# Graph attention in a decoder kernel: value weighting and normalisation moved between VectorE, ScalarE and GpSimd

## The reference, cut to what matters

```python
def _L2_attn_ref(h, Wl, Wr, att_l, att_r, Wf, ln_gamma, ln_beta):
    fl = (h @ Wl.T).reshape(b, n, H, HD).transpose(0, 2, 1, 3)      # H = 8, HD = 32
    fr = (h @ Wr.T).reshape(b, n, H, HD).transpose(0, 2, 1, 3)
    sl = einsum('bhnd,d->bhn', leaky(fl), att_l[0])
    sr = einsum('bhnd,d->bhn', leaky(fr), att_r[0])
    p = softmax(sl[:, :, :, None] + sr[:, :, None, :], axis=-1)
    ctx = einsum('bhnm,bhmd->bhnd', p, fr)
    y = h + ctx.transpose(0, 2, 1, 3).reshape(b, n, d) @ Wf.T
    mu, var = mean(y, -1), mean(square(y - mu), -1)
    return (y - mu) * rsqrt(var + 1e-05) * ln_gamma + ln_beta
x = x + _L2_attn_ref(layernorm(x), ...)
```

## Time and profile before

| what | value |
|---|---|
| median of 3 runs | 3631.68 us (3626.03 to 3635.91) |
| the profiled execution's own time | 3622.71 us |
| its span | 3620.9 us |
| TensorE busy in the whole span | 3182.0 us, 88% |
| VectorE | 1830.8 us, 51% |
| ScalarE | 1200.6 us, 33% |
| GpSimd | 917.2 us, 25% |
| mean granted TensorE clock | 0.939 |

### The profile page before, as it was taken

The page is one execution under the profiler, slowest core; times in us unless marked ns, Lnnn a source line. Parts: engine busy times, 40 slices in busy tenths (PEclk is TensorE's granted clock), DMA queues, the critical chain, the costliest instruction groups (busy, mean ns, idle before and its releaser), DMA issues. The chain is left out here.

```text
span 3620.9 us, 75209 instructions
## 1 busy us (share of the span) xinstructions
PE 3182.0 (88%) x30384; PEld 2203.4 (61%) x30384; DVE 1830.8 (51%) x4577; ACT 1200.6 (33%) x2371; POOL 917.2 (25%) x754
## 2 busy tenths in 40 slices
PE   8886999999977868878778999789996999899978
PEld 3334555555666854746545555489996886566655
DVE  7886544543233554332586666543334662455543
ACT  1222333333223432311225655322221652244332
POOL 1001533432000000423427878412111110104000
PEclk9998999999989989978889999889998999999989
DMA  4223000001042020634601110278886100111100
GB/s 150 58 67 97 9 9 17 8 8 32 18 55 24 4 52 4 182 99 125 180 18 33 34 30 21 76 269 333 332 323 222 38 8 6 61 49 53 42 9 15
DMA packets 173918, 287.21 MB, mean 79 GB/s; under 512 B 79120, under 2 KB 144197, under 8 KB 164274
## 3 DMA queue, kind: packets, MB, share of 16 engines
q1 hardware_dynamic: 166130, 262.48, 23.5%
q0 software_dynamic: 7488, 20.46, 1.7%
HBM read 244.49 MB, written 28.48 MB: 75 GB/s over the span
## 5 line engine op out<-in xcount | busy, mean ns | idle before, releaser
L2646 PE MATMUL ps<-L_ffn_xsT,arena 128*128 128x128 f32 x2584 | 309.9, 279 | 20.1 <-DVE L_ffn_xsT L2445 14.1
L2646 PEld LDWEIGHTS ps<-L_ffn_xsT,arena 128*128 128x128 f32 x2584 | 301.8, 196 | 23.8 <-DVE L_ffn_xsT L2445 16.8
L161 POOL TENSOR_TENSOR rstd<-nsc,mhalf 112x4 f32<-112x4 f32 (+1 forms) x24 | 40.1, 1669 | 919.6 <-DVE nsc L154 918.7
L820 POOL TENSOR_TENSOR L_xattn_rn<-L_xattn_ss,mhalf 125x16 f32<-125x16 f32 (+1 forms) x64 | 185.8, 2903 | 257.2 <-DVE L_xattn_ss L883 257.2
L3329 POOL TENSOR_TENSOR L_xattn_pT<-L_xattn_pT,L_xattn_keep 125x678 int32<-125x678 int32 x128 | 190.4, 1510 | 71.6 <-ACT L_xattn_pT L3584 71.6
L2544 ACT ACTIVATE L_ffn_silu<-ps,arena 128x128 f32<-128x128 f32 x280 | 102.9, 368 | 268.9 <-PE ps L2646 253.6
L701 PE MATMUL ps<-L_attn_prod,arena 128*32 128x448 f32 (+29 forms) x672 | 157.8, 507 | 27.3 <-DVE L_attn_prod L510 27.0
L2454 DVE SCALAR_TENSOR_TENSOR L_ffn_hT<-ps,arena,L_ffn_silu 128x128 f32<-128x128 f32 x280 | 97.9, 350 | 155.6 <-ACT L_ffn_silu L2544 155.4
L997 PE MATMUL ps<-arena,L_xattn_cT 128*125 128x512 f32 x384 | 166.1, 592 | 0.0
L2323 POOL DMA_INDIRECT L_ffn_rows_out<-L_ffn_ys,L_ffn_dest x78 | 79.7, 1022 | 335.5 <-DVE L_ffn_ys L2463 303.7
L2659 PE MATMUL ps<-arena,L_ffn_hT 128*128 128x256 f32 x646 | 154.1, 383 | 0.1
(11 more groups left out here) (585 smaller groups left out, 6873.1 us busy)
## 6 DMA issues: line engine op xcount, KB each, us to landing
arena<-in_L_ffn_up SPq DMA_DIRECT2D x35, 2056.0 KB
arena<-in_L_ffn_down SPq DMA_DIRECT2D x35, 1152.0 KB
L_xattn_ctxT<-in_ctxT SPq DMA_DIRECT2D x48, 375.0 KB, 3.7
arena<-in_L_ffn_up SPq DMA_DIRECT2D x43, 384.0 KB
L_attn_a<-L_attn_skew SPq DMA_DIRECT2D x16, 784.0 KB, 5.1
L_xattn_ctx<-in_ctx SPq DMA_DIRECT2D x30, 375.0 KB
arena<-L_xattn_kp SPq DMA_DIRECT2D x64, 93.8 KB, 3.3
L_xattn_mask<-in_mask SPq DMA_DIRECT2D x32, 164.1 KB, 8.4
```

Source lines behind the costliest of these rows:

```text
L820: nc.gpsimd.tensor_tensor(rn[0:r, i], ss[0:r, i], core.mhalf[0:r, 0:H], ALU.pow).then_inc(po_r.step("root", i), 1)
L2646: ins = nc.tensor.matmul(ps[:, 2 + b % 4, half * TS:(half + 1) * TS], self.up(i % WU, k, half * HM + m), xsT[:, i % 2, k], start=(k == 0), ...
```

## The change

Three things are moved in the second part of `L2Graph`, the rest of the program is as it was.

- `weighed(c)` goes from VectorE to GpSimd.
- The normalisation is split in three. ScalarE reads y from PSUM and computes `y * root - mean * root` into `yn` (L3136 in the changed kernel, one instruction for each batch, with two operands of one number per token). GpSimd multiplies `yn` by gamma (L2976). VectorE adds `yn` to `x` (L3055).
- For ScalarE's offset VectorE writes `minus`, the mean times -1 (L3048), behind the epsilon, and GpSimd multiplies it by the root into `less` (L2971).

TensorE's list keeps its order. Its waits now name other engines: `numerators(c)` waits for GpSimd's `weighed(c)`, and `result(c)` waits for ScalarE's read of the bank, `yn(c-3)`.

```diff
+            def weighed(c):
+                f = 2 * c // NH
+                pool.wait_ge(ac_w.sem, ac_w.at(f, "exp"))
+                pool.wait_ge(ac_r.sem, ac_r.at(2 * c + 1, "fr"))
+                if c >= 2:
+                    pool.wait_ge(pe_n.sem, pe_n.at(c - 2, "num"))
+                nc.gpsimd.tensor_tensor(by_head(wf[:, c % 2]), fr[:, 2 * c:2 * c + 2, :].rearrange("p n (h d) -> p (n h) d", d=HD),
+                                        pair_of(wa[:, :, 0], c), ALU.mult).then_inc(po_w.step("weighed"), 1)
+
+            def roots(c):
                 ln.pool(pool, ve_y, po, c)
+                if c >= 2:
+                    pool.wait_ge(ac_y.sem, ac_y.at(c - 2, "yn", 1))
+                pool.wait_ge(ve_y.sem, ve_y.at(c, "minus"))
+                pool.wait_ge(po.sem, po.at(c, "lnrs"))
+                nc.gpsimd.tensor_tensor(less[:, c % 2], minus[:, c % 2], ln.rs[:, :], ALU.mult).then_inc(po.step("lnmr"), 1)
+
+            def gains(c):
+                for u in range(2):
+                    pool.wait_ge(ac_y.sem, ac_y.at(c, "yn", u))
+                    nc.gpsimd.tensor_tensor(yn[:, c % 2, u * D:(u + 1) * D], yn[:, c % 2, u * D:(u + 1) * D], self.gam, ALU.mult).then_inc(po_g.step("gain", u), 1)
+            weighed(0)
+            weighed(1)
+            for c in range(PAIRS + 2):
+                if 2 <= c + 1 < PAIRS:
+                    weighed(c + 1)
+                if 0 <= c - 2:
+                    gains(c - 2)
+                if 0 <= c - 1 < PAIRS:
+                    roots(c - 1)
...
             def statistics(c):
                 bank = OUT[c % 3]
                 ln.vector(dve, ve_y, c, lambda u, q: ps[0:T, bank, u * D:(u + 1) * D], lambda u: dve.wait_ge(pe_o.sem, pe_o.at(c, "out")))
+                if c >= 2:
+                    dve.wait_ge(po.sem, po.at(c - 2, "lnmr"))
+                nc.vector.tensor_scalar(minus[:, c % 2], ln.mv[:, :, 0], -1.0, None, ALU.mult).then_inc(ve_y.step("minus"), 1)
 
             def result(c):
-                bank = OUT[c % 3]
-                dve.wait_ge(po.sem, po.at(c, "lnrs"))
-                for u in range(2):
-                    nc.vector.scalar_tensor_tensor(out=yn[:, c % 2, u * D:(u + 1) * D], in0=ps[0:T, bank, u * D:(u + 1) * D], scalar=ln.mv[:, u, 0:1], in1=self.gam,
-                                                   op0=ALU.subtract, op1=ALU.mult).then_inc(ve_a.step("gain", u), 1)
                 for u in range(2):
                     x = core.x[0:T, 2 * c + u, :]
-                    dve.wait_ge(ve_a.sem, ve_a.at(c, "gain", u))
+                    dve.wait_ge(po_g.sem, po_g.at(c, "gain", u))
                     dve.wait_ge(po_b.sem, po_b.at(2 * c + u, "shift"))
-                    nc.vector.scalar_tensor_tensor(out=x, in0=yn[:, c % 2, u * D:(u + 1) * D], scalar=ln.rs[:, u:u + 1], in1=x,
-                                                   op0=ALU.mult, op1=ALU.add).then_inc(ve_a.step("out", u), 1)
+                    nc.vector.tensor_tensor(x, x, yn[:, c % 2, u * D:(u + 1) * D], ALU.add).then_inc(ve_a.step("out", u), 1)
...
-            weighed(0)
             for c in range(PAIRS + 2):
                 if c < PAIRS:
                     contexts(c)
-                if c + 1 < PAIRS:
-                    weighed(c + 1)
...
+            def results(c):
+                bank = OUT[c % 3]
+                act.wait_ge(po.sem, po.at(c, "lnmr"))
+                if c >= 2:
+                    act.wait_ge(ve_a.sem, ve_a.at(c - 2, "out", 1))
+                for u in range(2):
+                    nc.scalar.activation(yn[:, c % 2, u * D:(u + 1) * D], ps[0:T, bank, u * D:(u + 1) * D], ACT.Identity,
+                                         bias=less[:, c % 2, u:u + 1], scale=ln.rs[:, u:u + 1]).then_inc(ac_y.step("yn", u), 1)
+            for c in range(PAIRS + 1):
+                if c < PAIRS:
+                    contexts(c)
                 if c == 1:
                     exps(1)
+                if c >= 1:
+                    results(c - 1)
```

## The result

| | before | after |
|---|---|---|
| median of 20 runs each | 3631.42 us (3626.03 to 3638.37) | 3638.98 us (3625.59 to 3654.31) |
| ratio after to before | | 1.0023 (95%: 1.0013 to 1.0032) |
| profiled execution, own time | 3622.71 | 3641.36 |
| its span, granted clock | 3620.9, 0.939 | 3639.3, 0.941 |

The kernel became 7.6 us slower (0.23%, just inside the 0.3% told of above; by the interval of the ratio it is 4.7 to 11.6 us); 3639.7 had been forecast. The profiled spans differ by more, 18.4 us: 7.4 of it is there before `L2Graph` begins (1795.85 before, 1803.21 after, in unchanged code), and some 4 us come after it. So the stage is compared by itself, from TensorE's first transposes of it to the first L197 of the next stage on VectorE, in three pieces.

A forecast was written before the change was run, and what follows sets the result against it. VectorE was taken to bound the loop's middle at 4.66 us a round; a dependent chain would replace it. Loop 11.7 us more, beginning 3.8 less: 8 slower, 3631.7 + 8 = 3639.7 us, range 3630 to 3648.

The forecast's parts named there:

- the loop: First statistics of y to the stage's end: eight chains plus 0.8 us, 50.7 for 39.0, 11.7 us more.
- the beginning: Up to the first statistics of y: 2.8 us from the unwaited first context, 1.5 from TensorE's clock.
- the first part: Up to the last sum by head: two early weightings over products L2967 lose about 0.5 us.
- the signs named: VectorE idle 2 to 3 us, L3041 6 to 6.5 apart, L2962 1.27, first context unwaited, TensorE idle about 2.
- The round: Pair loop: one chain from statistics to statistics, 6.5 us with a weighting and 5.8 without, against 4.66 before.
- What the weighting costs: GpSimd between root and gamma, pairs 0 to 4: 1.27 us, covering ScalarE's reads; without it one read, 0.55.
- Contention: VectorE's first addition to x beside GpSimd's second gamma product: 0.27 us per pair, bounds nothing and 0.39.
- Rival A: GpSimd's weighting is dear, its repeated operand costing as much again: 14 us slower, 3646; chance 0.17.
- Rival B: TensorE's clock falls inside the loop; half the pairs hit makes it 16 us slower, 3648; chance 0.06.
- Rival D: GpSimd's weighting isn't really ahead; TensorE waits under 1 us a round, inside slack, 3640 still; chance 0.04.
- Rival C: Pair loop: chain is covered, TensorE's 4.31 us round becomes the bound, 5 us faster, 3626; chance 0.11.
- The 0.36 in brackets: TensorE's wait for VectorE's context in its 4.67 us round before the change, leaving its own round 4.31.

The follow-up runs named there:

- norm late: Statistics first, with the seven small next-stage-mean instructions moved behind pair 6's addition: 3624.53 us against 3631.98 before, ratio 0.9983; repeated, 0.9979.
- statistics first: Changed kernel, with VectorE taking pair c-1's statistics ahead of pair c-2's addition to x: 3631.33 us against 3634.68 before, ratio 0.9992.

## Why the prediction was right

The forecast of 3639.7 us was 0.7 us from the median, and the mechanism is the one that it named: rounds one after another, each a closed chain. The terms were off in ways that partly cancel: the loop was forecast 2.8 us too long, the beginning gave 0.8 less than forecast, and the first part lost 1.1 more, which is not shown to come from the change. So the mechanism and the direction were earned, but a miss of 0.7 us is closer than the terms were, and closer than an interval of 4.7 to 11.6 us can tell: that much of it is luck. Of the signs named, VectorE's idle time (2.19) and the first context without a wait came out; TensorE's idle time (0.79 + 0.87) and the contexts' distance (5.98) fell just short, and L2962 took 1.05 for 1.27.

- **The round.** 6.5 was predicted and 5.98 measured. Term by term (the rows of the round above): statistics to the root 1.36 and 1.35 (1881.50 to 1882.85). Root and product 0.89, and 1.01 with the hand-over of 0.17 between them (0.86 from root to product, 0.15 to the next start). The weighting 1.27 and 1.01: this is the term that was mis-sized most. Gammas until the statistics of `x` 2.12 plus the hand-overs of 0.2, and 1.95. Statistics of `x` 0.66 and 0.66. Eight chains and the seven small operations came to 47.96 us (1856.67 to 1904.63) for 50.7; that is 8.9 more than before, for 11.7.
- **What the weighting costs.** Between a round with and one without it 0.7 was predicted; 0.29 was measured, and moving it back saved less still. The last rounds, 5.8 predicted, took 5.69. The reason is that ScalarE's reads run beside the weighting, as the prediction said, and take nearly as long: gamma starts 0.87 after the product with a read alone between them (1895.38 to 1896.25), and 1.16 with the weighting (1883.71 to 1884.87). Both terms were counted in the right place, but 1.27 against 0.55 was predicted, and 1.01 against 0.72 measured (0.87 less 0.15 for the product). The read by itself took 0.56.
- **Contention.** 0.27 a pair was taken; the additions lose 0.5 (0.76 to 1.26), but only some 0.17 of that is on the path (gammas to statistics 1.95, against 1.45 + 0.33 for a single addition behind both gammas). The rule of the Trainium skill ("SBUF — State Buffer", section "Who interferes with whom") held: additions with two inputs in SBUF stretched, while the context, with one, kept its 0.69 beside the root, and the statistics of "norm late" their 0.76 beside gamma. The forecast gave the rule without an exception that matters for other kernels: the same section excepts VectorE's two-port modes and names `tensor_scalar` among the operations that can enter them. L150 of "statistics first", such an instruction with one input, took 0.65 beside gamma for 0.17 alone; no run shows in which mode it ran. The sum without contention, 2.2 us smaller, would have been nearer for the loop (9.5 for 8.9 measured) and farther off for the stage (5.7 for 7.1).
- **The beginning.** The wait of the first context went, 2.8 as predicted. From TensorE's clock 1.5 was taken and 0.7 came. In the first part 0.5 was predicted for early weightings over products; one product shows it, 0.79 for 0.69. The part is 1.6 longer all the same. 1.0 of it had arisen before any moved instruction ran (from the start to TensorE's transposes behind its wait of 3.1 us: 33.68 before, 34.73 after), and 0.6 lies behind that, where TensorE ran most of its last products at half clock in this execution. TensorE, the last eight products of the first part, before and then after, and the clock after:

```profile
1831.82 3.74 PE L3135 MATMUL ps<-arena,L_attn_xT 128*112 128x512 f32 x8
```

```profile
1841.15 4.36 PE L3163 MATMUL ps<-arena,L_attn_xT 128*112 128x512 f32 x8
```

```profile
1840.00:1842.00 2.00, 2.00 (x7) 0.98 (x5) 1.66 (x3) 1.10 (x3) 1.56 (x2) 0.50 0.00 0
...
1867.00:1870.00 3.00, 3.00 (x9) 2.00 (x9) 2.90 (x13) 0.00 (x0) 0.44 (x1) 0.50 0.00 0
```

  The run with the weighting on VectorE has no early weighting and is as long there (45.37), and kernels with one lie between 43.5 and 46.3. So this is not shown to come from the change; when the clock falls within the stage differs between executions, and what sets that stays open.
- **Rival A** (dear weighting) fell: 1.05 us, less than an instruction with plain operands of its size (1.27). **Rival B**: the clock was low once inside the loop (the second row above); the four products with `Wf` took 1.91 us there for 1.03, inside TensorE's slack. In the steady rounds it is 1.00. **Rival D** was in fact there: TensorE waits 0.87 a round for a weighting issued in the same round, not a round ahead. The prediction placed that weighting wrongly, and was right that it costs nothing, as 0.79 us of slack are left behind it.
- **Rival C** had the decisive condition right (cover for the chain), and its price too low. TensorE's own round is not 4.31 but 3.91. The 0.36 in brackets is not all that a wait costs: the transposes behind it start 0.96 after the instruction ahead of them (1873.47 to 1874.43), 0.43 without a wait (1872.07 to 1872.50 in "norm late"), and the sum over tokens behind them starts after 0.60 for 0.38. So a round had 0.75 to give, which "norm late" collects.

## What to carry to other kernels

Before moving work off a busy engine, write down the dependent steps between two visits of that engine and what stands between them in its list: here 0.6 and 0.8 us of VectorE were freed, and a bare chain of 6 us took the place of a full engine of 4.7. The cure was the order, not the placement: with the statistics ahead of the addition the chain has a round beside it, and with the seven small operations out of the middle of the loop as well the same moves win. Doubling one cheap step is a good test: it grew every round by its full 0.47 while the chain was bare, and the steady ones by 0.26 or nothing when covered.

## What the runs showed of the hardware

- A product on GpSimd with an operand that repeats within its rows (112x512) took 1.05 us, less than one of 125x512 with plain operands, 1.27.
- VectorE's and GpSimd's instructions stretched each other where they overlapped: additions 0.76 to 1.26 for two, and to 2.12 with more of GpSimd's work behind; GpSimd's root 0.70 to 0.87 and its product of two numbers 0.20 to 0.41. Tiny VectorE operations suffered most for their size (0.17 to 0.91).
- At the start of the next stage a VectorE operation of 112x12 lasts 5.08 us while GpSimd fills buffers from 1905.74 to about 1911, in the kernel before too. No run tested whether the one makes the other. VectorE and GpSimd, kernel after:

```profile
1905.99 5.08 DVE L150 TENSOR_SCALAR mean<-nsc 112x12 f32<-112x12 f32 x1
```

```profile
1907.78 2.66 POOL L3363 MEMSET arena<- 125x3072 f32 x1
```
